# One row-tile border and seven routing borders moved, with normalization rows and a load order in the opening changed

## The reference, cut

```python
xn = _layernorm(x)
# edges
agg = segment_sum(xn[src] * edge_weight[:, None], dst) @ gnn_weight
# mix: k and v normed per head
dots = einsum('bhnd,bhne->bhde', k, v)
mixed = (einsum('bhnd,bhde->bhne', q, dots) / n) @ Wout.T + bout
x = x + agg + mixed
# experts, on the layer norm t of x
topk_vals, topk_idx = top_k(t @ gate_w + gate_b, 2)
h = relu(einsum('bsh,ehf->bsef', t, w1) + b1)
moe = sum(softmax(topk_vals) * select(h @ w2 + b2, topk_idx))
out = x + _layernorm(t + moe) * gamma + beta
```

## Time and profile before

| what | us |
|---|---|
| median of 3 runs | 1493.06 |
| lowest and highest run | 1493.06, 1496.05 |
| profiled execution, its own time | 1489.54 |
| its span, first to last instruction | 1487.7 |

### The profile page before, as it was taken

The page is one execution under the profiler, slowest core; times in us unless marked ns, Lnnn a source line. Parts: engine busy times, 40 slices in busy tenths (PEclk is TensorE's granted clock), DMA queues, the critical chain, the costliest instruction groups (busy, mean ns, idle before and its releaser), DMA issues. The chain is left out here.

```text
span 1487.7 us, 21903 instructions
## 1 busy us (share of the span) xinstructions
PE 1023.5 (69%) x6498; PEld 761.3 (51%) x6498; DVE 651.1 (44%) x2406; ACT 406.0 (27%) x1085; POOL 1007.7 (68%) x1094
## 2 busy tenths in 40 slices
PE   0099999997764889744199641896674997558880
PEld 0055555554542778522077520775553886447870
DVE  7545454443457422323223332225144233528776
ACT  4144343332121324201033210332221332214330
POOL 4477777777755767777777777777767774176734
PEclk9999999999977899956589865999886999889995
DMA  9676656733321998633489534895855985289883
GB/s 336 173 239 206 205 163 196 235 105 104 99 81 68 318 358 279 214 105 103 160 268 362 179 103 138 279 329 194 301 206 189 329 303 188 82 296 346 268 300 117
DMA packets 153597, 317.09 MB, mean 213 GB/s; under 512 B 24608, under 2 KB 97568, under 8 KB 153344
## 3 DMA queue, kind: packets, MB, share of 16 engines
q0 software_dynamic: 49296, 134.68, 28.9%
q1 hardware_dynamic: 64320, 142.25, 27.3%
q10 hardware_dynamic: 39856, 38.67, 7.7%
HBM read 251.15 MB, written 64.36 MB: 212 GB/s over the span
## 5 line engine op out<-in xcount | busy, mean ns | idle before, releaser
L873 POOL DMA_INDIRECT ring<-normed_rows,src_sb x831 | 799.4, 962 | 326.0 <-issue 286.5
L1528 PE MATMUL ps<-ring,S 128*32 128x256 f32 x1680 | 133.8, 462 | 233.0 <-DMA ring<-normed_rows,src_sb 148.2
L1664 PE MATMUL ps<-room 128*128 128x128 f32 x1872 | 240.1, 284 | 17.8 <-DMA room<-in_w1b 17.0
L1664 PEld LDWEIGHTS ps<-room 128*128 128x128 f32 x1872 | 228.4, 199 | 22.9 <-issue 20.6
L1677 PE MATMUL ps<-room 128*128 128x256 f32 x936 | 225.4, 384 | 9.2 <-issue 9.2
L1528 PEld LDWEIGHTS ps<-ring,S 128*32 128x32 f32 x1680 | 58.8, 126 | 281.4 <-issue 252.6
L1461 DVE TENSOR_TENSOR desk<-ps,room 128x256 f32<-128x256 f32 x121 | 51.2, 424 | 330.6 <-PE ps L1677 324.7
L1677 PEld LDWEIGHTS ps<-room 128*128 128x128 f32 x936 | 171.6, 194 | 30.9 <-issue 12.0
L1555 PE MATMUL ps<-room,tT 128*128 128x512 f32 x392 | 177.4, 595 | 0.0
L983 ACT ACTIVATE room<-ps,room 128x128 f32<-128x128 f32 x468 | 133.4, 368 | 122.7 <-PE ps L1664 122.7
L843 POOL DMA_INDIRECT rows_by_slot<-X,slot_i x98 | 96.1, 981 | 78.9 <-DVEq L1353 47.8
(11 more groups left out here) (226 smaller groups left out, 1176.5 us busy)
## 6 DMA issues: line engine op xcount, KB each, us to landing
room<-in_w2b SPq DMA_DIRECT2D x87, 640.0 KB, 6.6
room<-in_w1b SPq DMA_DIRECT2D x87, 514.0 KB, 5.7
room<-rows_by_slot SPq DMA_DIRECT2D x121, 128.0 KB
results_by_slot<-desk ACTq DMA_DIRECT2D x121, 128.0 KB
rows_by_slot<-desk ACTq DMA_DIRECT2D x6, 2432.0 KB
ring<-normed_rows,src_sb POOLq DMA_INDIRECT x831
normed_rows<-X SPq DMA_DIRECT2D x7, 896.0 KB, 7.7
result<-ring SPq DMA_DIRECT2D x49, 128.0 KB, 4.0
```

The lines of the kernel that those rows point to most:

```text
L873: pool.indirect_dma_start(out=ring[:, b % 2 * BT + m, :], out_offset=None, in_=table, in_offset=bass.IndirectOffsetOnAxis(ap=src_sb[:, b * ...
L1528: mm = pe.matmul(acc[w * W:(w + 1) * W, :], S[b % 2][:, m, :], ring[:, b % 2 * BT + m, :], start=(t == 0), stop=(t == GT - 1), skip_group_ ...
L1664: mm = pe.matmul(hps[g % 2][:, f * TS:(f + 1) * TS], w1_sb[g % WB][:, k * F + f * P:k * F + (f + 1) * P], xgT[g % 2][:, k, :], start=(k == ...
```

## The change

The part border moves from row tile 40 to 38; the seven segments end at 10, 20, 30, 38, 43, 46, 49 instead of 8, 16, 24, 32, 36, 40, 49. In the opening GpSimd normalizes the two rows per chunk that VectorE did; ScalarE takes a chunk's root ahead of the rows of the chunk before; edge weights and wkv are loaded behind the table's writes. In the tail loop closing steps are put only where no routing step is left.

```diff
+POOL_ROWS = CH - ACT_ROWS
-PT = (0, 40, NT)
-SUB = (0, 8, 16, 24, 32, 36, 40, NT)
+PT = (0, 38, NT)
+SUB = (0, 10, 20, 30, 38, 43, 46, NT)
...
             dve = max(dve, before_tile) + (RESULT_DVE if now > before_tile else 0.0)
+        if last in sent and not routes:
             if closing and dve < now + CLOSE_DVE:
...
-        CONSTS = [(ew[:, :], edge_w), (src_sb[:, :], src), (wkv_sb, wkv)]
+        CONSTS = [(src_sb[:, :], src)]
+        EDGE_CONSTS = [(ew[:, :], edge_w), (wkv_sb, wkv)]
...
                 sp.wait_ge(normed, ACT_ROWS * (c + 1))
-                sp.wait_ge(dve_normed, c + 1)
+                sp.wait_ge(pool_normed, POOL_ROWS * (c + 1))
                 sp.dma_start(rows_of(table, c * CH, CH), X2[:, c * CH:(c + 1) * CH, :]).then_inc(table_out, 16)
+            for o, i in EDGE_CONSTS:
+                sp.dma_start(o, i).then_inc(edge_consts_in, 16)
...
+            for c in range(NC):
+                pool.wait_ge(rstd_done, c + 1)
+                for q in range(c * CH + ACT_ROWS, (c + 1) * CH):
+                    pool.tensor_scalar(X2[:, q, :], X2[:, q, :], rstd[:, q:q + 1], nmr[:, q:q + 1],
+                                       ALU.mult, ALU.add).then_inc(pool_normed, 1)
...
-            for c in range(NC):
+            def root_chunk(c):
                 act.wait_ge(stats_done, c + 1)
...
+            root_chunk(0)
+            for c in range(NC):
+                if c + 1 < NC:
+                    root_chunk(c + 1)
                 act.wait_ge(rstd_done, c + 1)
...
-                for q in range(c * CH + ACT_ROWS, (c + 1) * CH):
-                    ins = dve.tensor_scalar(X2[:, q, :], X2[:, q, :], rstd[:, q:q + 1], nmr[:, q:q + 1],
-                                            ALU.mult, ALU.add)
-                ins.then_inc(dve_normed, 1)
...
-            dve.wait_ge(consts_in, 16 * len(CONSTS))
+            dve.wait_ge(edge_consts_in, 16 * len(EDGE_CONSTS))
```

More of the change, by code:

```diff
@@ L527, in gps_layer @@
         tables_in = sem("tables_in")
+        edge_consts_in = sem("edge_consts_in")
         later_in = sem("later_in")
@@ L533, in gps_layer @@
         normed = sem("normed")
-        dve_normed = sem("dve_normed")
+        pool_normed = sem("pool_normed")
         table_out = sem("table_out")
@@ L1704, in _ @@
             pe.wait_ge(normed, ACT_ROWS * NC)
-            pe.wait_ge(dve_normed, NC)
+            pe.wait_ge(pool_normed, POOL_ROWS * NC)
             pe.wait_ge(flag_ready, 1)
```

## The result

| | before | changed |
|---|---|---|
| median of 4 runs, us | 1494.55 | 1514.72 |
| lowest and highest, us | 1493.06, 1496.46 | 1509.67, 1517.53 |
| ratio to before, 95% interval | | 1.0138 (1.0102 to 1.0174) |
| profiled execution, its span, us | 1489.54, 1487.7 | 1509.67, 1507.9 |

A forecast was written before the change was run, and what follows sets the result against it. GpSimd's gathers (1.26 us each) set the pace to the last gather, then a chain through TensorE's expert tiles. Terms: +4.7 to the last gather, +16 tiles, +5.0 picks, sum +25.7, about 1518.5 us; range 1489 to 1536.

The forecast's parts named there:

- The opening: Before the first gather: VectorE loses 14 row normalizations and a 2.00 us wait for ScalarE; -6 us (from -3 to -6.6).
- Six more scatters: Before the last gather: 43 row tiles instead of 40 are scattered, 6 x 1.28 = +7.7 us.
- The first routing: GpSimd's waits around batch 25: routing 0 one slot later shortens one wait, lengthens its scatter's; -3 us (from -12 to 0).
- Later waits: Second half of the gathers: routings 4 and 5 between expert tiles make GpSimd wait more; +6 us (from 0 to +15).
- Expert tiles of the end: TensorE after the last gather: part 1 has 32 tiles with 27 weight loads, was 28 with 16; +16 us (0 to +31).
- Picks: Behind the last result: part 1 has 11 row tiles, not 9, so 22 picks instead of 18; +5.0 us.
- The closing rule: Tail loop: closing steps waiting for the last routing only change place between tiles; zero, within 2 us either way.
- Faster: Rival: DMA does not limit the end's tiles, 4.28 us each, and middle waits come out low; 1488 us, chance 0.15.
- Same: Rival: end tiles at a pace of 4.4 us with waits near their low ends; 1490 to 1496 us, chance 0.10.
- Slow rows on GpSimd: Rival: in the opening GpSimd's rows take above 1.85 us each and set the chunk; 1530 us at 3 us, chance 0.06.
- The starved GpSimd: Rival: routings 4 and 5 among tiles cost GpSimd 20 us of waits instead of 6; 1533 us, chance 0.09.
- The signs: Profile marks expected: first gather near 47.4, waits near 11 and 7.5, last gather near 1253, end intervals above 5 us.

## Why the prediction was right, point by point

- **The opening** (-6 forecast, -6.36 measured): right in its size and its parts. The roots' order and the moved constants gave 2.3 where 2.00 was read off the wait, and the rows 4.1 where 4.6 was worked out.
- **Six more scatters** (+7.7): counted, and they are there. Across executions they are met by shorter waits: from the first gather to the last it took 1195.2 to 1199.0 us in four profiles with the old borders (mean 1196.5) and 1191.9, 1196.6 and 1204.3 in three with the new (mean 1197.6). The -3.4 us of the table is thus partly this one execution; the mean says +1, 10 us better than the forecast of +10.7 instead of 14.
- **The first routing** (-3, from -12 to 0): right. GpSimd's waits up to 620 us (those above 0.6 us) sum to 33.0 us in the mean of those four profiles and to 28.4 in nine profiles of kernels whose first borders are 10 and 20.
- **Later waits** (+6, from 0 to +15): this step failed. The waits behind 620 us are 11.1 before and 6.9 after in the two profiles, 12.4 and 10.9 in the means: no loss. The step priced slots 64 and 65 at 24 and 28 us of TensorE work against 15.1 us of gathers, and passed 9 us on to GpSimd. The rows of the changed kernel, TensorE's edges around the two slots and GpSimd beside them:

```profile
1169.96 1.50 PE L1541 MATMUL ps<-ring,S 128*32 128x256 f32 x24
...
1191.83 1.50 PE L1541 MATMUL ps<-ring,S 128*32 128x256 f32 x24
...
1218.43 1.50 PE L1541 MATMUL ps<-ring,S 128*32 128x256 f32 x24
```

```profile
1184.58 1.00 POOL L855 DMA_INDIRECT rows_by_slot<-X,slot_i  x1 [0.30 <-issue]
...
1197.55 0.99 POOL L885 DMA_INDIRECT ring<-normed_rows,src_sb  x1 [0.30 <-issue]
...
1220.24 0.94 POOL L885 DMA_INDIRECT ring<-normed_rows,src_sb  x1 [2.71 <-PE ps L1541]
```

  The slot with four tiles takes 21.87 us and the one with five tiles and a mix 26.60, 48.5 together where 52 were taken, so the slots were priced nearly right. But GpSimd puts routing 4's ten scatters, 13 us, between the same two slots, asks for no gather meanwhile, and then waits 2.71 us instead of 9 (2.2 to 2.7 at this place in the four profiles with that routing). A transfer that occupies the bound engine is slack for the engine behind it; the step had not set the one against the other. That the scatters are the reason is read off these rows; no run moved them.
- **Expert tiles of the end** (+16, from 0 to +31): right in mechanism, 9 us too small in the profile. The price of a load, taken as 1.26, measured 1.23 in the kernel's time; of the changed kernel's 33 us in the profile 27 are pace (154.1 against 126.6 us from first tile to last) and 6 a later start, so the close agreement is partly luck. The start was 65.8 instead of 62, since routing 5's steps on VectorE put the last rank 3.2 us later than taken, and the first weights are asked for only at 1297.22, when ScalarE is past part 0's last stores (SyncE waits 48.2 us for it). The pace term missed that a run begins anew. At the first break TensorE works off both layer 2 of the pair before it turns the next rows (1314.20); at the second those rows are asked for too late, as shown above. That costs 3.9 and 10.0 us. They were not in the sum, and the 4.6 and 5.3 taken for the first fourteen intervals covered them by luck: 71.4 us were forecast there and 73.2 measured (1304.78 to 1378.02), but the eleven intervals inside the second and third run took 4.37 each. In all it was 154 us against 150.
- **Picks** (+5.0): 5.3 measured. **The closing rule** (0): nothing changes.
- **The rivals.** *Faster* needed a mean pace below 4.4; it was 4.97 over all 31 intervals and 4.68 in the longest run. *Same* took a pace of 4.4 too. Slow rows on GpSimd: 0.54 us, no. The starved GpSimd: its waits behind 620 us did not grow, no.
- **The signs.** The first gather, the waits of 10.33 and 7.42, the scatters, the waits for w1b and the full DMA came as listed. The last gather was to stand near 1253 and ended at 1238.99 (near 1245 with the mean of the middle), and intervals above 5 us came only here and there. Waits vanishing in the middle was named as a sign of being wrong; it came true for the term on later waits, and the end outweighed it.

So the total held for two reasons: the mechanism that decides (loads in part 1, from which 16 of 20.6 us come) was the right one at the right price, within what the ratios can tell, and two smaller errors of opposite sign, -14 in the middle (-10 in the means) and +9 at the end, partly cancelled. That cancelling, and with it the 3.8 us, is luck.

## What to carry to other kernels

Splitting the last segment makes its work start earlier, but each piece begins with its own weights and its own empty pipeline; where DMA is full at the end (0.97 to 1.00 here), count loads before tiles. A forecast of waits for a bound engine has to set its own other work (here scatters) against the work it is said to wait for. And parts of a change are worth measuring apart: here the opening and the first borders, alone, make a kernel of 1480 us out of a change that costs 20.

## What the runs showed of the hardware

GpSimd's `tensor_scalar` on 128x256 floats took 0.54 us, VectorE's 0.37, 1.5 times. Beside it VectorE's statistics did not slow down: seven took 2.38 us without GpSimd's rows and with them, and chunks followed at 3.71 us with two rows on GpSimd and with four. The Trainium skill (Perfetto Trace Analysis, Optimizing Scalar/DVE Operations) warns that moving work between these two might not help, since they share a read port of SBUF. Here it helped by 4.1 us of the 4.6 expected, and what is missing shows in VectorE's steps right behind the statistics, with the rows still running on GpSimd and without:

```profile
34.11 0.49 DVE L1060 CAST desk<-desk 128x280 f32<-128x280 int32 x1 [0.19 <-issue]
...
35.17 0.56 DVE L1064 TENSOR_TENSOR desk<-desk 128x280 f32<-128x280 f32 x1
35.82 0.41 DVE L1066 TENSOR_SCALAR desk<-desk 128x70 f32<-128x70 f32 x1
```

```profile
38.67 0.30 DVE L1057 CAST desk<-desk 128x280 f32<-128x280 int32 x1
...
39.55 0.45 DVE L1061 TENSOR_TENSOR desk<-desk 128x280 f32<-128x280 f32 x1
40.08 0.22 DVE L1063 TENSOR_SCALAR desk<-desk 128x70 f32<-128x70 f32 x1
```

The cast, the subtraction and the small scaling are 0.19, 0.11 and 0.19 us longer beside GpSimd, together 0.49. GpSimd's rows slow down there too: the last four take 2.81 us (33.35 to 36.16), 0.70 each. That this is the port was not tried.
